# A sandwich of attention and a mixture of experts: the rotation of queries and keys moved into a PSUM bank of its own, and the low parts dealt out anew

## The reference, cut to what matters

```
x = x + layernorm(attention(layernorm(x)))
x = x + layernorm(experts(layernorm(x)))

attention: h = layernorm(x) * scale + bias
  c_q = h @ w_down_q.T ; c_kv = h @ w_down_kv.T          (64 wide each)
  q = rope(c_q @ w_up_q.T) ; k = rope(c_kv @ w_up_k.T)   (16 heads of 64)
  v = c_kv @ w_up_v.T
  out = softmax(q k.T / 8) v ; out @ w_out.T + residual
  rope: rot[2i] = e*cos - o*sin ; rot[2i+1] = e*sin + o*cos
experts: 8 experts, 2 chosen per token by softmax of logits,
  each down(silu(gate(x)) * up(x)), weighed by a softmax of the two
```

## Time and profile before

| | us |
|---|---|
| median of 3 runs | 1504.33 |
| lowest, highest | 1504.27, 1508.53 |
| span of the profiled execution (the only time shown of it) | 1526.2 |
| PE busy | 1417.3 (93%) |
| DVE busy | 1206.0 (79%) |
| ACT busy | 1066.9 (70%) |
| POOL busy | 1234.6 (81%) |

### The profile page before, as it was taken

How to read it: one execution, slowest core, us unless ns; L and a number is a source line. 1 busy time by engine, 2 the same in 40 slices (tenths; PEclk the granted TensorE clock), 3 DMA queues, 4 the chain that set the end, 5 groups by cost and what they waited for, 6 DMA issues and landing times. The chain is left out here.

```text
span 1526.2 us, 45381 instructions
## 1 busy us (share of the span) xinstructions
PE 1417.3 (93%) x17868; PEld 938.4 (61%) x17868; DVE 1206.0 (79%) x2687; ACT 1066.9 (70%) x2072; POOL 1234.6 (81%) x729
## 2 busy tenths in 40 slices
PE   4899999999999999998999999989999999799985
PEld 1366666666666666665666655656666565599774
DVE  7788887877788788887788789888887888865456
ACT  2777788778878777777778777767877776534334
POOL 5588998989888988996888988979889889543464
PEclk8799999999999999999999999999999999999987
DMA  5444445543233233332333233323332351143112
GB/s 170 117 112 141 139 140 143 164 129 78 71 89 85 54 78 102 81 82 64 93 82 93 74 81 95 81 65 78 79 88 64 77 175 47 47 125 91 45 53 58
DMA packets 104083, 142.34 MB, mean 93 GB/s; under 512 B 16960, under 2 KB 51520, under 8 KB 103488
## 3 DMA queue, kind: packets, MB, share of 16 engines
q1 hardware_dynamic: 100800, 133.13, 32.0%
q0 software_dynamic: 3072, 6.30, 1.4%
HBM read 20.49 MB, written 24.38 MB: 29 GB/s over the span
## 5 line engine op out<-in xcount | busy, mean ns | idle before, releaser
L1245 ACT ACTIVATE probs<-psum 128x512 f32<-128x512 f32 x1024 | 614.6, 603 | 200.0 <-PE psum L955 198.5
L1993 POOL TENSOR_TENSOR probs_lo<-probs 128x1024 f16<-128x1024 f32 x299 | 635.6, 2136 | 116.1 <-ACT probs L1245 114.7
L974 PE MATMUL psum<-cv,probs 128*128 128x66 f16 x4096 | 477.8, 193 | 15.2 <-POOL probs_lo L1993 8.6
L1541 DVE CUSTOM_DVE_ANT_0 scan_out<-psum,ahead 128x512 f16<-128x512 f32 x512 | 348.3, 685 | 168.4 <-PE psum L849 160.1
L976 PE MATMUL psum<-cv,probs 128*128 128x64 f16 x4096 | 477.2, 194 | 0.0
L978 PE MATMUL psum<-cv,probs_lo 128*128 128x66 f16 x4096 | 475.9, 192 | 0.0
L976 PEld LDWEIGHTS psum<-cv,probs 128*128 128x128 bf16 x4096 | 381.3, 98 | 110.7 <-issue 3.7
L974 PEld LDWEIGHTS psum<-cv,probs 128*128 128x128 bf16 x4096 | 386.1, 98 | 78.5 <-POOL probs_lo L1993 14.1
L953 PE MATMUL psum<-q_both,k_twice 128*128 128x512 f16 x1024 | 389.7, 381 | 3.1 <-ACT probs L1245 3.1
L955 PE MATMUL psum<-q_max,k_ones 65*128 65x512 f16 x1024 | 392.0, 383 | 0.0
L978 PEld LDWEIGHTS psum<-cv,probs_lo 128*128 128x128 f16 x4096 | 380.8, 98 | 0.0
(11 more groups left out here) (224 smaller groups left out, 1927.1 us busy)
## 6 DMA issues: line engine op xcount, KB each, us to landing
t_swapped<-t_sin SPq DMA_DIRECT2D x248, 128.0 KB, 2.0
k_twice<-qk_hi SPq DMA_DIRECT2D x128, 128.0 KB
slots<-oacc SPq DMA_DIRECT2D x25, 512.0 KB, 3.1
q_lone<-qk_hi SPq DMA_DIRECT2D x64, 128.0 KB, 2.3
q_both<-qk_hi SPq DMA_DIRECT2D x64, 128.0 KB
q_both<-qk_lo SPq DMA_DIRECT2D x64, 128.0 KB
q_max<-qk_hi SPq DMA_DIRECT2D x64, 128.0 KB
k_ones<-qk_lo SPq DMA_DIRECT2D x64, 128.0 KB
```

The costliest lines, as they stand in the source:

```text
L974: pe.matmul(acc, high[:, q * P:(q + 1) * P, 1], v[:, 0:VLO], start=opens, stop=False, skip_group_check=True)
L1245: act.activation(probs[s % 4][:, i, :], score_ps[tile % SCORE_BANKS], ACT.Exp, scale=SCALE).then_inc(probs_done, 1)
L1541: dve.tensor_tensor_reduce(scan_out[m % 2][:], bank[BANK_OF["base", n, m]], ahead[m % 2][:], 1.0, LOWEST, ALU.add, ALU.max, max_all[a][:, ...
L1993: pool.tensor_tensor(probs_lo[s % 4][:].rearrange("p a n -> p (a n)"), p, p.bitcast(BF16).rearrange("p (n two) -> p n two", two=2)[:, :, 1 ...
```

## The change

- PSUM: 2 banks for scores (a tile now waits for the tile two places before), 3 for jobs, and one for the rotation of groups 2 and later (`ROPE_BANK`). The job order over the three banks leaves those projections out. A projection waits instead for the low part of the quarter before (`lows_rotated`).
- Rotation of groups 2 and later, quarter by quarter in that bank: projections in steps 0, 4, 8, 12. DVE multiplies by sine into `t_sin`, waits for that, multiplies by cosine in place, and two steps later (2, 6, 10, 14) subtracts the swapped rows in place, ahead of its scan of the step. ACT rounds to float16 in that same step. DVE forms the low part one step later (3, 7, 11, 15). POOL's `rope_add` and `low_rotated` are gone from the groups.
- `key_difference` reads the float16 keys in place of float32.
- Low parts: DVE in steps 4, 8, 12 (before 2, 4, 6, 8, 10, 12, and 14 in the sending groups), POOL in the other 13. The last two groups keep their lists.
- Sends: two in each of groups 14 to 29 (steps 5 and 15), then in the odd steps of the last two groups (16 there, before 24).
- SP: `put_lone` in two halves with a wait each (four DMAs where two were), the swaps moved in SP's order. One transpose of the next batch moves from step 12 to 13.

```diff
-SCORE_BANKS, JOB_BANKS = 3, 3
+SCORE_BANKS, JOB_BANKS = 2, 3
+ROPE_BANK = JOB_BANKS
-PROJ_STEPS = (0, 2, 4, 6)
-ROPE_STEPS = (3, 5, 7, 9)
-HIGH_STEPS = (4, 6, 8, 10)
+PROJ_STEPS = (0, 4, 8, 12)
+SUM_STEPS = (2, 6, 10, 14)
+LOW_ROTATED_STEPS = (3, 7, 11, 15)
 DIFF_STEP = 8
-LOW_ROTATED_STEPS = (11, 13)
-DVE_STEPS = (2, 4, 6, 8, 10, 12)
-SENDING = (14, 15, 17, 18, 19, 20, 21, 22, 23, 26, 27, 28, 29)
-LATE_DVE_STEPS = {**{g: DVE_STEPS + (14,) for g in SENDING}, GROUPS - 2: ...
+DVE_STEPS = (4, 8, 12)
+SENDING = range(14, 30)
+LATE_DVE_STEPS = {GROUPS - 2: (1, 3, 5, 7, 9, 11, 13, 15), GROUPS - 1: ...
+def place_jobs():
+    banks, before, last, turn = {}, {}, {}, 0
+    for job in FRONT_JOBS + ATTENTION_JOBS:
+        if job[0] == "proj" and job[1] >= 2:
+            at = ROPE_BANK
+        else:
+            at, turn = turn % JOB_BANKS, turn + 1
+        banks[job], before[job], last[at] = at, last.get(at), job
-SEND_AT = [(g, s) for g in SENDING for s in ((15,) if g in (19, 27) else (5, 15))]
-SEND_AT += [(g, s) for g in (30, 31) for s in range(STEPS) if s % 4 < 3]
+SEND_AT = [(g, s) for g in SENDING for s in (5, 15)]
+SEND_AT += [(g, s) for g in (30, 31) for s in range(1, STEPS, 2)]
...
 def rotate(n, j):
-                if n >= 2 and t == 0:
-                    dve.wait_ge(qk_lo_done, 2 * (n - 1 if n == 2 else n) - a)
-                dve.tensor_tensor(rotated(n, a, t), src, cos_sb[:, cols], ALU.mult)
+                if n < 2:
+                    dve.tensor_tensor(rotated(n, j), src, cos_sb[:, cols], ALU.mult)
...
                 dve.tensor_tensor(swap_from(n, j), src, sin_sb[:, cols], ALU.mult).then_inc(proj_taken, 1)
+                if n >= 2:
+                    dve.wait_ge(proj_taken, 4 * n + (j + 1))
+                    dve.tensor_tensor(src, src, cos_sb[:, cols], ALU.mult).then_inc(cos_done, 1)
+            def rope_sum_in_bank(n, j):
+                dve.wait_ge(cos_done, 4 * (n - 2) + (j + 1))
+                dve.wait_ge(swap_in[swap_slot(n, j)], swaps_in(n, j))
+                dve.tensor_tensor(bank[ROPE_BANK], bank[ROPE_BANK], swap_to(n, j), ALU.subtract).then_inc(rope_sum, 1)
+            def low_rotated(n, j):
+                dve.wait_ge(qk_hi_done, 4 * n + (j + 1))
+                dve.tensor_tensor(qk_lo[n % 2][a][:, cols], bank[ROPE_BANK], qk_hi[n % 2][a][:, cols],
+                                  ALU.subtract).then_inc(qk_lo_done, 1)
...
 ACT, step s
-                    if g < LAST - 1 and s in HIGH_STEPS:
-                        split_rotated(g + 2, HIGH_STEPS.index(s))
+                    if g < LAST - 1 and s in SUM_STEPS:
+                        split_rotated(g + 2, SUM_STEPS.index(s))
 DVE, step s
+                    if g < LAST - 1 and s in SUM_STEPS:
+                        rope_sum_in_bank(g + 2, SUM_STEPS.index(s))
                     lagged(g, s, g > 0)
                     if g < LAST:
                         scan(g + 1, s)
+                    if g < LAST - 1 and s in LOW_ROTATED_STEPS:
+                        low_rotated(g + 2, LOW_ROTATED_STEPS.index(s))
 POOL, step s
-                    if g < LAST - 1:
-                        if s in ROPE_STEPS:
-                            rope_add(g + 2, ROPE_STEPS.index(s))
-                        for a in (1, 0):
-                            if s == LOW_ROTATED_STEPS[1 - a]:
-                                low_rotated(g + 2, a)
```

More of the change, by code:

```diff
@@ L102, in front_at @@
     k = 4 if b == 1 else 0
-    return {**{("norm", t): (k, 2 + t) for t in range(TILES)}, ("x", 0): (k, 11), ("x", 1): (k, 12),
+    return {**{("norm", t): (k, 2 + t) for t in range(TILES)}, ("x", 0): (k, 11), ("x", 1): (k, 13),
             ("latent", 0): (k, 14), ("latent", 1): (k, 15), ("rows", 0): (6, 14)}
@@ L156 @@
 FRONT_JOBS = FRONT_PROJ[0] + FRONT_PROJ[1] + FRONT_SCANS[0] + FRONT_TURNS[:1] + FRONT_SCANS[1] + FRONT_TURNS[1:]
-IN_ORDER = FRONT_JOBS + [job for g in range(GROUPS) for s in range(STEPS) for _, job in jobs_in(g, s)]
-BANK_OF = {job: k % JOB_BANKS for k, job in enumerate(IN_ORDER)}
-BEFORE = {job: IN_ORDER[k - JOB_BANKS] if k >= JOB_BANKS else None for k, job in enumerate(IN_ORDER)}
+ATTENTION_JOBS = [job for g in range(GROUPS) for s in range(STEPS) for _, job in jobs_in(g, s)]
+def place_jobs():
[6 more added lines that the diff above has]
+        banks[job], before[job], last[at] = at, last.get(at), job
+    return banks, before
+BANK_OF, BEFORE = place_jobs()
 def dve_steps(g):
@@ L286, in program @@
         score_ps = [psum[:, i] for i in range(SCORE_BANKS)]
-        bank = [psum[:, SCORE_BANKS + i] for i in range(JOB_BANKS)]
+        bank = [psum[:, SCORE_BANKS + i] for i in range(JOB_BANKS + 1)]
         outacc = psum[:, 6:8]
@@ L465, in swap_to, with rotated @@
             return t if swap_slot(n, j) >= 2 else t[:]
-        def rotated(n, a, t):
-            return rot_second[a][t] if n == 1 else rot[a][:, t * HALF:(t + 1) * HALF]
+        def rotated(n, j):
+            if n >= 2:
+                return bank[ROPE_BANK]
+            a, t = PROJ[j]
+            return rot_second[a][t] if n else rot[a][:, t * HALF:(t + 1) * HALF]
         def z_rows_of(n):
@@ L613, in put, with put_lone @@
                 sp.dma_start(dst, src[h * DH:(h + 1) * DH, :]).then_inc(signal, 16)
-            def put_lone(n):
-                sp.wait_ge(qk_hi_done, 4 * n + 4)
+            def put_lone(n, half):
+                cols = slice(half * HALF, (half + 1) * HALF)
+                sp.wait_ge(qk_hi_done, 4 * n + 3 + half)
                 if n >= 2:
@@ L619, in put_lone @@
                 for h in range(2):
[L620 removed]
+                    put(q_lone[n % 2][h][h * DH:(h + 1) * DH, cols], qk_hi[n % 2][0][:, cols], h, lone_in[half])
             def put_both(n, h):
@@ L706, in _ @@
             sp.wait_ge(fills_done, FILLS)
-            put_lone(0)
+            put_lone(0, 0)
+            put_lone(0, 1)
             swap_rows(1, 2)
@@ L713, in _ @@
             put_rows(0, 0)
-            put_lone(1)
+            put_lone(1, 0)
+            put_lone(1, 1)
             put_rows(0, 1)
@@ L754, in _ @@
                 if g < LAST - 1:
-                    put_lone(g + 2)
+                    put_lone(g + 2, 0)
+                    swap_rows(g + 2, 3)
                 clear_slots(g, 3)
@@ L760, in _ @@
                     load_value_weights(g + 2)
+                if g < LAST - 1:
+                    put_lone(g + 2, 1)
             put_score(LAST, 1)
@@ L791, in free @@
                 kind, n, at = before
-                if kind == "proj":
+                if kind == "proj" and n >= 2:
+                    pe.wait_ge(qk_lo_done, lows_rotated(n, at))
+                elif kind == "proj":
                     pe.wait_ge(proj_taken, 4 * n + (at + 1))
@@ L1975, in rope_add @@
                 pool.wait_ge(swap_in[swap_slot(n, j)], swaps_in(n, j))
-                part = rotated(n, a, t)
+                part = rotated(n, j)
                 pool.tensor_tensor(part, part, swap_to(n, j), ALU.subtract).then_inc(rope_sum, 1)
```

42 lines of the change are left out of this document (26 added, 16 removed).

## The result

The changed kernel takes 1523.32 us in the median of 4 runs (1520.63 to 1525.79); the kernel before, run beside it, 1504.35 us (1504.27 to 1508.53). The ratio is 1.0119, with a 95% interval of 1.0101 to 1.0136: 19 us slower, where 7 us faster was forecast. It also lies outside the range.

The account below looks back on a forecast made before the run. PE's own work, busy for 93% of the span, was taken as the bound, so only its stalls could change. -23 - 3 + 14 + 3 + 2 = -7 us gave span 1519, median 1497; range 1482 to 1520.

Parts of the forecast that it names:

- step 3: Job banks: projections leave the rotation of three banks, so PE waits less on DVE's scans; -23 us (ends 0, -36).
- step 4: POOL's run of seven low parts falls behind, but hidden from PE; -3 us (ends -10, +10).
- step 6: DVE's sum now waits for the swap's DMA; one in ten late, half passed on: +3 us (ends 0, +12).
- rival B: Slower: POOL's backlog of seven low parts in a row keeps DVE out; +32 us, 1529; chance 0.08.
- step 5: Two score banks cost nothing except at the square roots, 2.35 us in six groups: +14 us (ends +5, +20).
- step 1: DVE's load: net +0.3 us in a plain group, -1.4 in a sending one; busy share unchanged.
- step 2: Shared side of SBUF: POOL gets free time, so DVE's three low parts fall from 1.72 to 1.2 to 1.5 us.
- C: No change: half of step 3's gain (-15) against +19 of costs, less POOL's gain; 1504 to 1505; chance 0.21.
- D: Faster still: waits on scans nearly vanish (-33) and roots cost only the bank (+5); 1478; chance 0.12.
- A: Slower: ACT waits for DVE's sums past 2.7 us into their step, PE loses 0.8 per group; +23, 1520; chance 0.22.

Follow-up runs that it names:

- first and third set: Follow-up runs grouped by chip; the kernel before took 1504.96 us in the first set and 1504.99 in the third.
- second set: Follow-up runs of edited versions of the changed kernel on another chip, where the kernel before took 1529.29 us.

## Why the prediction was wrong

The bookkeeping, by one profile each of the 32 groups; the measured term of a row is the difference from the row above it:

| | groups, us | step | written, us | measured, us |
|---|---|---|---|---|
| kernel before without roots | 1270.0 | | | |
| changed, roots on GpSimd, loads later | 1249.1 | 3 and 4 | -26 | -21 |
| changed, roots on GpSimd | 1256.0 | 6 | +3 | +7 |
| changed, without roots | 1264.1 | none (rival B) | 0 | +8 |
| changed | 1287.4 | 5 | +14 | +23, less 1.5 that before's roots cost |

The sum is +16 in the groups. With step 5 alone put right, the forecast would have been +1 us, so the other rows had their part in the miss. The experts' part adds 2.1 where +2 had been written for small things. The fourth row is what the held key difference of groups 19 and 27 costs in the run without roots. In the changed kernel itself only group 19's is held, with a gap of 3.2 us and 1.7 us of clock behind it; counted by that, it is 5 us, and the roots have the other 3. The experts' 2.1 us don't look like the last send's: with nothing but two score banks, and before's sends, that part is 2.0 us longer as well. Why is open.

**Step 5, two score banks: the step that failed most.** The mechanism and the six places were right: the score tile waits in groups 10, 11, 18, 19, 26 and 27, at step 4. The standing still was nearly right as well: PE's waits there rose from 2.8 to 19.3 us, by 16.5 where 14 was written, 5 of them by the bank alone. The term was mis-sized, 14 us for 22 (18 if only the six root groups are counted), in two ways.
- The prediction priced PE's standing still and let it go on at full speed after it. In the changed kernel every gap of 3 us or more in the groups was followed by a stretch at 1.2 GHz. Turning the roots off takes 22.0 us off the six groups, and 6.9 of them are PE's busy time (246.5 to 239.6). The earlier trace rows had the same stall of 4 us, and I charged it with 4.0; its group has a clock of 0.96 in the first profile and 0.92 in the second. I wrote that I'd be wrong at the root if PE's busy time or clock moved, and had not looked at where the clock moves already.
- I let a late swap and a root fall on different places. A gap of 2.35 + 0.7 = 3.05 us had been worked out, and groups 11 and 19 have just that, group 26 has 2.82. In groups 10, 18 and 27 the gap is 3.3, 3.9 and 4.0: there the swap of step 2 landed 3.9, 4.4 and 4.5 us after the sine product's end, DVE's sum waited for it, ACT's rounding for the sum, and the root for the rounding. In group 18 ACT stood idle for 1.5 us ahead of the rounding, and 1.0 of them is the swap. Step 6 charged late swaps apart from the roots. That these three late swaps make the difference was not tried by itself.

**Rival B, a collision of DVE and POOL: a term that the sum put at nothing.** Step 4 called the fourth group of a batch as tight as before, and step 1 took the key difference as undelayed. B's mechanism came there, at another instruction than the one it named. Here is group 19 of the changed kernel, DVE's key difference and then what POOL did meanwhile:

```profile
847.07 4.63 DVE L1581 TENSOR_TENSOR k_diff<-qk_hi 128x512 f16<-128x512 f16 x1
```

```profile
847.31 1.03 POOL L2073 TENSOR_TENSOR res_sb<-x_sb,ln_mv 128x512 f32<-128x512 f32 x1
848.31 1.88 POOL L2045 TENSOR_TENSOR probs_lo<-probs 128x1024 f16<-128x1024 f32 x1
850.16 1.25 POOL L2054 TENSOR_TENSOR oacc<-oacc,o_part 128x512 f32<-128x512 f32 x1
```

The key difference has its median at 0.415 us. PE lost 3.2 us at step 10 there. The same happens in group 19 in all four other profiles of the changed kernel with three low parts and with roots on ACT or none; with six low parts, a low part is held in its place. With the roots on GpSimd no key difference of the groups passes 1.0 us; why the timing then differs in just this way was not tried, and the DVE reciprocals that went with the roots are one candidate. The Trainium skill ("SBUF — State Buffer", Who interferes with whom) lets the second to issue wait until the first finishes; here three instructions of POOL in a row passed a waiting one of DVE, so the rule gives too low a bound.

**Step 3, job banks.** -23 was written. Its signs came: waits on max_all 6.2 us where under 10 was written, L833's share gone, DVE's low part at 1.42 us (under 1.5 was written), POOL's at 2.00 (just not under 2.0), none of DVE's over 3.4. With step 4 it gave 21 for 26, only seen once roots, swaps and the held key difference are out of the way. What is missing went into new waits: 7.5 us at step 13.5, where the base tile waits for a job bank that the residual's additions hold because these now stand behind a rotation. My walk through a group was a plain group's, and had no additions in it.

**Step 6, late swaps.** +3 was written and about 7 measured, within its ends. But I spread it over all swaps as chance. DVE did stand idle for a swap at 32 places, 26.1 us in all, but PE lost over 2 us only at those of groups 6 and 14, whose projection is in step 0, behind the loads of x in SP's queue. I had asked whether SP's own steps had room, not which other DMA stands ahead of a transfer that now has a deadline.

**Steps 1, 2 and 4** held for plain groups. The sums took 0.692 us, the cosine product in place 0.699, the low rotated parts 0.686; the float16 key difference 0.415 where 0.7 was taken.

**Rivals.** C (no change) and D didn't come. A's time came (1520), but not for A's reason: its sign came without its cost. The sums ended 2.1 us into their step in the median of 120, counted from the step's first score tile, but 34 of them ended past the 2.7 from which A was to decide, more than one per group. Yet of L982's 30.2 us, 19.3 stand at step 4 of the root groups and 5.2 in groups 6 and 14; under 6 us are left for all others, where A had 23. B's low parts of 5 us didn't come in the changed kernel, but its collision did, as told above; the time of 1529 and the half of the sending groups did not.

## What to carry to other kernels

A stall has a second price: look at the granted clock behind each long stall of the profile before, and charge it to every stall that you expect to be longer. When a buffer is taken away from a stream, go to the places where its producer does something rare (a table load, a norm) and walk these places, not the plain step. And ask whether the rare work can leave that engine: here the same change was 1.2% slower with the roots on ScalarE and 0.8% faster with them on GpSimd, which the change itself had freed. Look at the longest instruction of a kind and not only at its mean: the mean of the low parts stayed at 1.42 us while two of them took over 6.

## What was not expected of the hardware

- In the groups of the changed kernel every gap of 3.0 us or more on PE was followed by a stretch at 1.2 GHz (a clock of 0.50). Shorter gaps went either way: with the root ahead, one of 2.26 us was followed by it in group 11 and not in groups 10, 18 and 26; one of 2.82 us in group 26 was not followed by it in the changed kernel, and was with later loads.
- A DVE instruction with two SBUF inputs, the key difference, took 4.63 us beside three instructions of POOL that began after it; 28 of the 32 took 0.42 us. A low part took 6.43 and 6.62 us in two other runs.
- GpSimd's power of -0.5 on 128x8 takes 1.67 us, against 2.86 us on ACT for two table loads and a root (1.28 + 0.30 + 1.28), and delays no exponential.
- The experts' part took 173 to 177 us in all profiles of the first and third set and 192 to 199 in those of the second set, on another chip, with the same code in that part. The kernel before itself has 195.2 in one profile and 173.3 in another. The difference between such profiles is more than the whole effect studied.
